# The first expert block is taken out of PSUM and split during attention's last stretch, and four engine orders are rewritten

## What is computed

```python
# L0: group norm, one-head attention over 256 positions, residual
# L1: squeeze 1x1 -> relu -> expand 1x1 and 3x3 -> relu, residual, then tokens
# L2: layer norm, 8-head attention (window 64, causal), residual;
#     layer norm, quantized product with a binarized 128x128 weight, residual
# L3: layer norm, 8-head causal attention, residual;
#     layer norm, router over 8 experts, the two best of each token:
for e in range(E):                        # E = 8, hidden width 512
    h = relu(x @ W1[e] + b1[e])           # 128 -> 512
    y = h @ W2[e] + b2[e]                 # 512 -> 128
    out += gate[:, e] * y                 # zero unless e is among the two best
```

## Time and profile before

| | us |
|---|---|
| median of 3 runs (238.41 to 238.84) | 238.69 |
| the profiled execution | 238.59 |
| its span, first to last instruction | 236.8 |
| TensorE busy | 225.3 |
| VectorE busy | 204.7 |
| ScalarE busy | 168.1 |
| GpSimd busy | 92.1 |

### The profile page before, as it was taken

One profiled execution on the slowest core, in us unless ns is written; L12 is line 12 of the kernel. 1 busy time (PEld: TensorE's weight loads), 2 busy tenths in 40 slices (PEclk: granted clock), 3 DMA queues, 4 the chain that ended last, 5 costly groups with the idle time before them and its releaser, 6 DMA issues.

```text
span 236.8 us, 4624 instructions
## 1 busy us (share of the span) xinstructions
PE 225.3 (95%) x1495; PEld 172.5 (73%) x1495; DVE 204.7 (86%) x524; ACT 168.1 (71%) x498; POOL 92.1 (39%) x155
## 2 busy tenths in 40 slices
PE   7899898999999999999999998999999999999995
PEld 2697566677776687676876675887888888888885
DVE  4678889985989989999798965999999996799986
ACT  2276355899769997799969968666557766666660
POOL 6200325668885856277825819924200000000000
PEclk9999999999999999999999999999999999999999
DMA  6910000000310300030000303510110002612001
GB/s 177 373 45 4 0 0 0 1 3 14 121 47 4 89 0 3 0 93 0 3 1 0 91 1 116 155 44 28 55 53 0 3 0 79 190 44 79 13 1 44
DMA packets 9463, 11.71 MB, mean 49 GB/s; under 512 B 720, under 2 KB 6096, under 8 KB 9312
## 3 DMA queue, kind: packets, MB, share of 16 engines
q1 hardware_dynamic: 9008, 11.16, 15.3%
q10 hardware_dynamic: 432, 0.27, 0.4%
HBM read 10.87 MB, written 0.56 MB: 48 GB/s over the span
## 4 chain that ended last, share of the span: by engine, by line
PE 61%; DVE 14%; ACT 9%; POOL 9%; DMA 3%; issue 3%; SPq 1%; POOLq 0%; ACTq 0%; DVEq 0%
PE bank L1031 6%; PE bank L1046 6%; PE bank L1043 6%; PE bank L1044 6%; PE bank L1033 6%; PE bank L1032 6%; ACT early_prob L588 4%; PE bank L955 4%; DVE negmax L1475 4%; POOL w_lo L434 3%; DMA pk<-packed 3%; PE bank L980 2%; PE bank L889 2%; PE bank L931 2%; POOL w_hi L432 2%
## 5 line engine op out<-in xcount | busy, mean ns | idle before, releaser
L821 ACT ACTIVATE hb<-bank,pk 128x512 f32<-128x512 f32 x64 | 43.0, 710 | 19.6 <-PE bank L1033 19.6
L1853 DVE TENSOR_TENSOR hlo<-hb,hhi 128x512 fp32r<-128x512 f32 x64 | 46.1, 741 | 4.8 <-ACT hhi L824 3.7
L588 ACT ACTIVATE prob<-bank,negmax 128x192 f32<-128x192 f32 (+1 forms) x64 | 28.8, 480 | 5.5 <-DVE negmax L1475 5.2
L1475 DVE TENSOR_REDUCE negmax<-bank 128x2 f32<-128x384 f32 (+2 forms) x48 | 29.8, 640 | 2.7 <-PE bank L937 2.3
L544 ACT ACTIVATE probT<-bank 128x512 f32<-128x512 f32 x38 | 23.0, 639 | 5.9 <-PE bank L955 4.3
L1031 PE MATMUL bank<-xhi,w_hi 128*128 128x512 f32 x64 | 25.6, 399 | 1.2 <-ACT hhi L824 1.1
L434 POOL TENSOR_TENSOR w_lo<-w_raw,w_hi 128x256 fp32r<-128x256 f32 x32 | 25.2, 788 | 2.6
L1043 PE MATMUL bank<-hhi,w_hi 128*128 128x512 f32 (+2 forms) x68 | 25.9, 381 | 0.0
L1046 PE MATMUL bank<-hlo,w_hi 128*128 128x512 f32 (+2 forms) x68 | 25.9, 381 | 0.0
L1044 PE MATMUL bank<-hhi,w_lo 128*128 128x512 f32 (+2 forms) x68 | 25.8, 380 | 0.0
L1033 PE MATMUL bank<-xhi,w_lo 128*128 128x512 f32 x64 | 25.0, 390 | 0.0
(11 more groups left out here) (159 smaller groups left out, 525.2 us busy)
## 6 DMA issues: line engine op xcount, KB each, us to landing
w_raw<-w SPq DMA_DIRECT2D x16, 256.0 KB, 3.1
comb_b<-routes SPq DMA_DIRECT2D x16, 256.0 KB, 3.2
pk<-packed SPq DMA_DIRECT2D x1, 1280.0 KB, 8.9
pk<-packed SPq DMA_DIRECT2D x1, 560.0 KB, 6.3
xs<-x SPq DMA_DIRECT2D x3, 128.0 KB, 2.6
out<-acc SPq DMA_DIRECT2D x3, 128.0 KB, 1.7
xs<-x ACTq DMA_DIRECT2D x1, 128.0 KB, 3.0
pk<-packed ACTq DMA_DIRECT2D x1, 68.0 KB, 2.5
```

Of the source, the lines that this page charges most:

```text
L588: last = nc.scalar.activation(prob_of(n, u)[:, of], lane[n][u % 2][:, of], ACT.Exp, bias=negmax[n][:, unit_query(u), h:h + 1], accum_out=s ...
L821: nc.scalar.activation(hb[blk % 2][:, j, :], h_bank[j][:, :], ACT.Relu, bias=bias).then_inc(h_ready, 1)
L1475: V.tensor_reduce(negmax[n][:, unit_query(u), heads[0]:heads[-1] + 1], lane[n][u % 2][:, :].rearrange("q (h k) -> q h k", h=len(heads))[:, ...
L1853: V.tensor_tensor(hlo[blk % 2][:, j, :], hb[blk % 2][:, j, :], hhi[blk % 2][:, j, :].bitcast(F32), ALU.subtract).then_inc(hlo_ready, 1)
```

## The change

probT is allocated in front of early_prob. ScalarE's hidden takes a range of chunks, and its four chunks of block 0 are called inside attention's list; VectorE's split_hidden of block 0 also, the first with a wait for the last transposes of sequences 2 and 3. TensorE's last list has turn_routes(0) earlier and two chunks of hidden(0) later. exp_of_gap and gates(0) come earlier. Besides, many neighbours in the four lists change places, from the convolution on, mostly at 85 to 103 us and at 112 to 126 us, and one keep_clock filler goes. The functions are the same otherwise, and so is every matmul.

```diff
@@ allocation
         prob = each("prob", [128, 2, 512], scope=attention_memory)
+        probT = each("probT", [128, 2, 512], scope=attention_memory)
         early_prob = each("early_prob", [128, 512], n=2, scope=attention_memory)
-        probT = each("probT", [128, 2, 512], scope=attention_memory)
@@ ScalarE, middle
-            probs_turned(0, 3, 5)
             upper_keys(1, 1)
             upper_keys(1, 0)
+            probs_turned(0, 2, 5)
+            masked_keys(1, 1, 0)
+            probs_turned(0, 3, 5)
+            upper_queries(1, 0)
+            inverse_sums_turned(0, 2)
+            upper_queries(1, 1)
             inverse_sums_turned(0, 3)
-            masked_keys(1, 1, 0)
-            upper_queries(1, 0)
             masked_keys(1, 1, 1)
-            upper_queries(1, 1)
-            probs_turned(0, 2, 5)
             exps(1, 0, 0)
-            inverse_sums_turned(0, 2)
             exps(1, 1, 0)
+            probs_turned(1, 0, 0)
             probs_turned(1, 1, 0)
             exps(1, 1, 1)
-            probs_turned(1, 0, 0)
             turned(1, 3)
...
@@ ScalarE, end of attention
             probs_turned(1, 2, 3)
+            exp_of_gap(0)
             exps(1, 3, 5)
+            hidden(0, range(0, 1))
             exps(1, 2, 5)
-            exp_of_gap(0)
             probs_turned(1, 3, 5)
+            turn_routes(0)
             probs_turned(1, 2, 5)
-            turn_routes(0)
+            hidden(0, range(1, 2))
+            hidden(0, range(2, 3))
+            inverse_sums_turned(1, 2)
             inverse_sums_turned(1, 3)
-            inverse_sums_turned(1, 2)
...
+            hidden(0, range(3, 4))
+
+            for blk in range(1, BLOCKS):
@@ TensorE, convolution
             squeeze(0)
+            group_stats(1, 1)
             squeeze(1)
-            group_stats(1, 1)
-            keep_clock(rest_a, 1)
@@ TensorE, middle
-            turn_probs(0, 3, 5)
             project_keys(1, 1)
             project_keys(1, 0)
-            turn_inverse_sums(0, 3)
             turn_probs(0, 2, 5)
+            turn_probs(0, 3, 5)
             project_queries(1, 0)
             values(1, 1)
+            turn_inverse_sums(0, 2)
             project_queries(1, 1)
+            turn_inverse_sums(0, 3)
             mix(0, PAIRS[1], 4)
+            mix(0, PAIRS[1], 5)
+            scores(1, 0, 0)
+            scores(1, 1, 0)
+            project_out(0, 3)
+            project_out(0, 2)
+            scores(1, 1, 1)
             values(1, 0)
-            scores(1, 0, 0)
-            mix(0, PAIRS[1], 5)
-            scores(1, 1, 0)
-            turn_inverse_sums(0, 2)
-            project_out(0, 3)
-            scores(1, 0, 1)
-            scores(1, 1, 1)
-            project_out(0, 2)
+            turn_probs(1, 0, 0)
             turn_probs(1, 1, 0)
             scores(1, 1, 2)
+            scores(1, 0, 1)
+            mix(1, PAIRS[0], 0)
+            turn(1, 3)
             scores(1, 0, 2)
-            turn_probs(1, 0, 0)
-            turn(1, 3)
...
@@ TensorE, late
             project_keys(1, 3)
+            project_keys(1, 2)
             turn_probs(1, 0, 5)
-            project_keys(1, 2)
...
@@ TensorE, end of attention
             turn_probs(1, 2, 4)
+            turn_routes(0)
             turn_probs(1, 3, 5)
+            mix(1, PAIRS[1], 4)
+            turn_probs(1, 2, 5)
             hidden(0, range(1, 2))
             hidden(0, range(2, 3))
-            turn_probs(1, 2, 5)
-            turn_routes(0)
-            mix(1, PAIRS[1], 4)
+            turn_inverse_sums(1, 3)
             mix(1, PAIRS[1], 5)
-            turn_inverse_sums(1, 3)
             turn_inverse_sums(1, 2)
             hidden(0, range(3, 4))
@@ VectorE, split_hidden
+                if blk == 0 and chunks[0] == 0:
+                    for n in PAIRS[1]:
+                        dve.wait_ge(pT_full[n], 2 * UNITS)
@@ VectorE, middle
             copy_values(1, 1)
+            masked_keys(1, 0, 1)
             lower_queries(1, 0)
-            masked_keys(1, 0, 1)
             lower_queries(1, 1)
+            normalize(0, 3)
+            normalize(0, 2)
             largest(1, 0, 0)
-            normalize(0, 3)
-            copy_values(1, 0)
             largest(1, 1, 0)
             add_attention(0, 3)
-            normalize(0, 2)
+            add_attention(0, 2)
             norm_variance([3])
+            copy_values(1, 0)
             largest(1, 1, 1)
-            add_attention(0, 2)
...
@@ VectorE, late
+            lower_queries(1, 3)
             normalize(1, 1)
-            lower_queries(1, 3)
+            copy_values(1, 2)
             largest(1, 2, 0)
-            copy_values(1, 2)
+            largest(1, 3, 0)
             normalize(1, 0)
-            largest(1, 3, 0)
...
@@ VectorE, end of attention
             largest(1, 3, 5)
+            gates(0)
             copy_probs(1, 3, 4)
             copy_probs(1, 2, 4)
-            gates(0)
             inverse_sums(1, 2)
             inverse_sums(1, 3)
+            split_hidden(0, range(0, 1))
+            split_hidden(0, range(1, 2))
+            split_hidden(0, range(2, 3))
+            normalize(1, 3)
+            normalize(1, 2)
+            split_hidden(0, range(3, 4))
...
-            split_hidden(0, range(1))
-            for n in PAIRS[1]:
-                normalize(1, n)
-            split_hidden(0, range(1, HC))
```

More of the change, by code:

```diff
@@ L607, in turn_routes, with hidden @@
                 copy(combT[:, h * 512:(h + 1) * 512], r_bank[h][0:E, :]).then_inc(combT_ready, 1)
+            def hidden(blk, chunks=range(HC)):
+                e = blk % E
+                if blk >= 2:
+                    act.wait_ge(y_full, blk - 1)
+                for j in chunks:
+                    act.wait_ge(h_full, blk * HC + j + 1)
+                    bias = const("b1", e * HC + j, e * HC + j + 1)
+                    nc.scalar.activation(hb[blk % 2][:, j, :], h_bank[j][:, :], ACT.Relu, bias=bias
+                                         ).then_inc(h_ready, 1)
+                    if j % 2 == 0:
+                        nc.scalar.activation(hhi[blk % 2][:, j, :], h_bank[j][:, :], ACT.Relu, bias=bias
+                                             ).then_inc(hhi_ready[0], 1)
             def inverse_sums_turned(a, n):
@@ L768, in _ @@
             exps(1, 1, 4)
+            exps(1, 0, 4)
             probs_turned(1, 0, 3)
-            exps(1, 0, 4)
             exps(1, 1, 5)
@@ L1174, in _ @@
             values(0, 1)
+            scores(0, 0, 0)
             scores(0, 1, 0)
-            scores(0, 0, 0)
             scores(0, 1, 1)
             scores(0, 0, 1)
+            turn_probs(0, 0, 0)
+            scores(0, 0, 2)
             turn_probs(0, 1, 0)
             scores(0, 1, 2)
-            turn_probs(0, 0, 0)
-            scores(0, 0, 2)
             scores(0, 1, 3)
+            mix(0, PAIRS[0], 0)
             turn(0, 2)
-            mix(0, PAIRS[0], 0)
             turn(0, 3)
@@ L1277, in _ @@
             turn_probs(1, 1, 1)
+            scores(1, 1, 4)
+            product(1, 2)
             scores(1, 0, 4)
-            product(1, 2)
-            scores(1, 1, 4)
             turn_probs(1, 1, 2)
@@ L1315, in _ @@
             scores(1, 3, 2)
+            scores(1, 2, 3)
             turn_probs(1, 2, 0)
+            turn(3, 1)
             scores(1, 3, 3)
-            turn(3, 1)
-            scores(1, 2, 3)
             mix(1, PAIRS[1], 0)
@@ L1510, in gates, with split_hidden @@
                 V.tensor_tensor(comb[:, of, :], comb[:, of, :], oneh[:, of, :], ALU.add).then_inc(comb_ready, 1)
+            def split_hidden(blk, chunks=range(HC)):
+                if blk >= 2 and chunks[0] == 0:
+                    dve.wait_ge(y_full, blk - 1)
+                if blk == 0 and chunks[0] == 0:
+                    for n in PAIRS[1]:
+                        dve.wait_ge(pT_full[n], 2 * UNITS)
+                for j in chunks:
+                    dve.wait_ge(h_ready, blk * HC + j + 1)
+                    if j % 2 == 1:
+                        V.tensor_copy(hhi[blk % 2][:, j, :], hb[blk % 2][:, j, :]).then_inc(hhi_ready[1], 1)
+                    dve.wait_ge(hhi_ready[j % 2], blk * HC // 2 + j // 2 + 1)
+                    V.tensor_tensor(hlo[blk % 2][:, j, :], hb[blk % 2][:, j, :], hhi[blk % 2][:, j, :].bitcast(F32),
+                                    ALU.subtract).then_inc(hlo_ready, 1)
             def copy_probs(a, n, u):
@@ L1782, in _ @@
             largest(1, 0, 1)
+            largest(1, 1, 2)
+            norm(1, 2)
             largest(1, 0, 2)
-            norm(1, 2)
-            largest(1, 1, 2)
             add_bias(3)
@@ L1788, in _ @@
             quantize(3)
+            largest(1, 1, 4)
+            add_bias(2)
             largest(1, 0, 3)
-            add_bias(2)
-            largest(1, 1, 4)
             quantize(2)
```

86 lines of the change are left out of this document (31 added, 55 removed).

## The result

The changed kernel took 236.72 us (median of four runs; 238.58 before, measured beside it), a ratio of 0.9917, interval 0.9902 to 0.9932: faster by 2.0 us by the ratio and by 1.9 by the medians, where 2.3 was forecast. One of the four runs was slow (239.85 us, granted clock 0.986) and stays out of the ratio. Its profiled execution spans 235.1 us, before 236.8. TensorE's busy share is the same, 95%, and its clock digit is 9 throughout, as in the earlier trace rows.

What follows compares the result with a forecast made beforehand. After 85 us TensorE's own work plus a few holes was taken as the bound. 1.25 + 0.75 + 0.45 = 2.45, less 0.15 for hidden waits, gave 2.3 off the 238.69 median: 236.4 us, range 235.5 to 237.9.

Steps and rivals of the forecast that it cites:

- the hand-over: Attention to experts: block 1 begins 0.98 us sooner and a 0.27 us hole goes, 1.25 us gained.
- the middle: Reordered 85 to 103 us: ScalarE's exponentials begin at 96.6 and end sooner, 0.75 us gained, bounds 0 and 0.9.
- the late part: Reordered 112 to 126 us: TensorE's hole before 125.93 shrinks, 0.45 us gained, bounds 0 and 0.6.
- the start: First 50 us: nothing moves, taken as 0, bounds a gain and a loss of 0.3 us.
- the experts: After 150 us: hole at 162.81 may go, gain at most 0.35 us, not counted; slow subtractions lose 0 to 0.3.
- Split 3 to 145.8: Hand-over: VectorE's last split of block 0 ends at 145.8 us; down(0) needs the last hlo at 149.9.
- ScalarE's next exponentials come about 0.5 sooner: Late part: the second maximum ends at about 120.4 instead of 121.2, so the exponentials come about 0.5 us sooner.
- An unchanged length from down(0) to the end: Experts: a sign that the forecast is right, the length from down(0) to the end staying 88.1 us.
- (a): Rival: only the hand-over pays, middle and late orders no better than the old; 237.45 us, 237.8 with contention; chance 0.20.
- (b): Rival, middle: VectorE's later copy_values of sequence 0 delays scores(1,0,1); 239.5 us if 3.0 us late; chance 0.07.
- (c): Rival, hand-over: ScalarE becomes the bound, five more activations (2.85 us) before rT; 237.6 us; chance 0.14.
- (d): Rival, convolution: the clock falls for want of the filler at 27, about 3 us more; 239.4 us; chance 0.02.

Runs made afterwards that it cites:

- e1: The kernel before with only the hand-over part (buffers, block 0's chunked hidden and split_hidden, the lists' ends): 236.75 us, ratio 0.9922.
- e8: The kernel before with the hand-over part and the reordered middle (85 to 103 us), start and late part as before: 236.15 us, ratio 0.9881.
- e4: The changed kernel with one TensorE swap undone, mix(1, PAIRS[0], 3) in front of turn(2,3) again: 236.47 us, ratio 0.9925.
- e5: The changed kernel with the first 50 us as before and two pairs of steps near 110 us back in old order: 236.08 us, ratio 0.9886.
- e10: The kernel before with the hand-over part, but gates, routes and their exponential behind the unit-5 exponentials, probability copies and turn_probs(1,2,5): 237.9 us, ratio 0.9962.
- e2: The changed kernel without its hand-over part, only the rewritten orders up to 126 us: 238.67 us, ratio 1.0004.
- e9: The kernel before with the hand-over part, but only chunk 0 ahead of rT on ScalarE, normalizations ahead of splits 1 to 3: 237.48 us, ratio 0.9936.
- e3: The changed kernel with the lists of the first 50 us as before, filler included: 236.32 us, ratio 0.9912.

## Why the prediction was right, and where it was not

The total and the sign held, and so did the two largest terms, the hand-over and the middle. The rest was off: the late part by 0.72 us and the start by 0.36, against 0.54 in the experts and 0.17 in the hand-over. That these errors nearly cancelled, to 2.08 us where 2.30 was forecast, is in part luck.

- **Hand-over: 1.25 forecast, 1.42 measured.** The mechanism is the one forecast, and e1 shows it alone. Block 1 starts 0.96 us sooner from hidden(0) (8.68 to 7.72 us; forecast 0.98), and the 0.27 us hole is gone. Most of the missing 0.19 is the restart behind a hole: before, the first product behind each of the two holes is followed after 0.31 and 0.30 us (144.68 to 144.99, 146.42 to 146.72), in the changed kernel after 0.24 and 0.23. I counted each hole's length and not that. "Split 3 to 145.8" was wrong in size: it ended at 147.20, with the subtractions at up to 1.22 us each, and down(0) did not wait for it.
- **Middle: 0.75 forecast, 0.74 measured** at the 108 mark, and 0.73 in e8 by itself. ScalarE's 1.19 us before the turned probabilities is 0.40 at 96.24. The exponentials behind them begin at 97.22, forecast 96.6; most of that is the later start, for in e8, which has the old start, they begin 59.44 us behind turn(0,1), and the forecast was 59.51.
- **Late part: +0.45 forecast, −0.27 measured.** Two errors. "Bounds 0 and 0.6": I looked at 112 to 126 only, but the hunk begins near 108 and moves turn(2,3) ahead of a mix and an exponential unit ahead of a copy; that costs 0.48, and e4 and e5 show both causes. And "ScalarE's next exponentials come about 0.5 sooner" came to half: from turn(0,1) the second maximum ends 0.57 us sooner, but those exponentials begin 0.26 sooner (121.38, before 121.30), since they now stand directly behind the unit in front of them. The hole of 0.63 us by the pitch before 125.93 became two of 0.24 (124.28 and 126.16 in the changed kernel), and from 112 to 126 the change won 0.21 us, not 0.45.
- **First 50 us: 0 with bounds of 0.3 forecast, −0.36 measured.** Walking the queues "with present durations" was the step that failed: the new order moves VectorE's products against GpSimd's by some tenths of a microsecond, and their durations change. I had the same effect in the experts' bound and did not carry it here. The filler cost nothing: the convolution's twelve matmuls take 2.86 us, as before, and no digit of the clock fell.
- **Experts: 0, at most +0.35 forecast, +0.54 measured.** "An unchanged length from down(0) to the end" was wrong. The hole at 162.81 closed (0.51 us to it from the matmul before, changed 0.23), the transposes behind it begin their last 0.76 us after their first instead of 0.90 (162.81 to 163.71), and a step of 0.30 at 162.00 is 0.23 again. The lead that I named for it, VectorE's, is the cause: it writes ht 1.78 us earlier against TensorE, and the table behind e10 shows the length following it. What failed is the size: I took only the hole of 0.3, and left out the slower transposes behind it and the step before it.
- **The page on the shared port.** The Trainium skill, "GPSIMD Engine Reference", section 8 (Key points), says that GpSimd contends with VectorE instructions that have two SBUF inputs; the trace agrees: 0.68 to 0.69 us alone, 0.81 to 1.00 beside GpSimd at the start. What I made of it, that each of block 0's four subtractions would be slow, did not come: they took 0.68, 0.77, 1.22 and 0.77 us. Beside the first, at 141.07, GpSimd's cast was the slow one (141.06 to 142.01, 0.95 us instead of 0.40); the slowest lay beside GpSimd's subtraction w_lo (143.43 to 144.50). No block of the experts lost time to it.
- **Rivals.** (a), only the hand-over pays, describes the net (e2: nothing) and not the cause. (b): vh was copied at 96.17 and the scores it could hold up began at 96.99 without a wait. (c): ScalarE had chunk 0's bank and both exponential units done by 139.8, and turn_probs(1,2,5), at 140.20, did not wait. (d): no clock digit fell.

## What to carry to other kernels

When one engine's list hands over from one stage to the next, empty the next stage's first buffers from inside the old stage's list, where the engine has slack, and check for each step pulled forward what now stands behind it on the other engines: two neighbours swapped near 110 us took back two thirds of what a whole stretch of reordering had won. A queue walked with the present durations is good to a tenth or two only where VectorE's and GpSimd's neighbours keep their places against each other; a shift of some tenths of a microsecond there cost 0.31 us in one product. And compare stretches from a mark behind the start: that tells 0.1 us where the run times tell 0.3 to 0.9.

## What was not expected of the hardware

A hole costs TensorE more than its length: the second product behind it starts 0.30 to 0.32 us after the first instead of 0.23 (before 144.68 and 146.42; e9 145.84). The same 0.31 to 0.34 us stands behind the first product after transposes or mixes, with no hole (101.66 and 105.57 us from turn(0,1) in the kernel before).

Between VectorE and GpSimd it matters which is under way when the other begins, and either can be the slow one. A VectorE subtraction or kM product that begins while a GpSimd weight split or kM product has more than 0.15 us to run ends 0.53 to 0.56 us behind the end of that GpSimd row. In the changed kernel: kM 43.15 behind 42.62, kM 45.40 behind 44.86, hlo 143.90 behind 143.35, hlo 145.05 behind 144.50 (this one took 1.22 us). A GpSimd one that begins 0.12 to 0.45 us behind VectorE's takes longer in its turn: kM 0.91 us instead of 0.48, w_lo 1.05 to 1.16 instead of 0.73. Where both begin within 0.05 us either can be the slow one: GpSimd's cast at 141.06, VectorE's product at 42.15. VectorE's cast with one input is slowed too, to 0.78 us at 142.32, where it takes 0.41 at 146.12 in the kernel before. That one waits for the other fits these rows; it is read from them and was not tried by itself.

All thirteen profiled executions begin with TensorE at the lower of its two levels (1.2 of 2.4 GHz): the bf16 fillers take 0.63 us there. In twelve of them products take the short durations of the upper level (0.38 us for a filler or a 128x256 product) from a point between 5 and 10 us on. Two ran the first attention at half speed, e5 and e8. The pairs of 128x256 products of the first attention, first e1, then e5:

```profile
10.91 0.59 PE L1062 MATMUL bank<-hn,pk 128*128 128x256 f32 x2
...
12.64 0.59 PE L1062 MATMUL bank<-hn,pk 128*128 128x256 f32 x2
```

```profile
10.33 1.06 PE L1062 MATMUL bank<-hn,pk 128*128 128x256 f32 x2
...
12.89 1.06 PE L1062 MATMUL bank<-hn,pk 128*128 128x256 f32 x2
```

e8 has the same 1.06 us. Its granted clock reads 0.50 from 8 to 14 us, behind a hole of 1.43 us at 7.96, and its products are at full speed from 14.8 us on; e3 has a hole of 1.30 us at 8.61 and keeps the full level. e5 has no such hole: its products take the long durations from the start and the short ones only from 14.1 us on. Its clock row reads 1.00 all the time, because the trace has no clock entry before 13.9 us and the page counts what has none as full. The two executions took 2.3 and 3.0 us longer than the median of their kernel (238.40 and 239.18 us). What kept or brought the lower level was not tried. So something like my rival (d) exists, but elsewhere, and e8 and e5 give no sign that the change has a part in it; and the clock row alone doesn't exclude it, the duration of a known product does.
